# Two groups of the feed forward inside the drain of each attention layer, and the last two norms by a power on GpSimd

## The reference, cut to what matters

```
for l in range(2):
    h = shift_token(x)                                 # half the features come from the token before
    q, k, v = split(h @ wqkv[l])                       # 8 heads of 64
    o = local_attention(rotary(l2norm(q)), rotary(l2norm(k)), v)   # windows of 64 tokens
    x = x + o @ wo[l]
    h = shift_token(x)
    h = (h - mean) / sqrt(var + 1e-5) * ln_g[l] + ln_b[l]
    a, g = split(h @ w1[l] + b1[l])                    # 341 + 341 columns
    x = x + (a * gelu(g)) @ w2[l] + b2[l]
```

## Time and profile before

| | |
|---|---|
| median of 3 executions | 504.55 us (504.04 to 505.84) |
| profiled execution, its own time | 507.01 us |
| its span, first to last instruction | 505.1 us |
| PE busy | 435.7 us, 86% |
| weight loads | 302.5 us, 60% |
| DVE busy | 354.5 us, 70% |
| ACT busy | 313.4 us, 62% |
| POOL busy | 256.5 us, 51% |
| mean granted clock of PE | 0.947 |

### The profile page before, as it was taken

The page is one execution under the profiler, slowest core; times in us unless marked ns, Lnnn a source line. Parts: engine busy times, 40 slices in busy tenths (PEclk is TensorE's granted clock), DMA queues, the critical chain, the costliest instruction groups (busy, mean ns, idle before and its releaser), DMA issues.

```text
span 505.1 us, 13155 instructions
## 1 busy us (share of the span) xinstructions
PE 435.7 (86%) x4851; PEld 302.5 (60%) x4851; DVE 354.5 (70%) x733; ACT 313.4 (62%) x698; POOL 256.5 (51%) x225
## 2 busy tenths in 40 slices
PE   4899897749899999999885998989999999885993
PEld 2566565415677776766652665767667676672563
DVE  3687867265888888888642356689888898842556
ACT  2787676326677787877635244768778787651424
POOL 4578877465656666566440015565665656610002
PEclk9999899668999999999898999899999999989797
DMA  6900000000000000000000000000000000000002
GB/s 177 328 6 3 3 3 1 1 1 2 6 6 12 9 9 9 7 14 7 8 10 6 0 1 1 5 10 6 11 8 7 13 7 11 8 9 9 0 1 83
DMA packets 21038, 10.36 MB, mean 21 GB/s; under 512 B 13236, under 2 KB 20208, under 8 KB 20976
## 3 DMA queue, kind: packets, MB, share of 16 engines
q1 hardware_dynamic: 20400, 9.14, 6.7%
q10 hardware_dynamic: 576, 0.39, 0.2%
HBM read 6.38 MB, written 1.05 MB: 15 GB/s over the span
## 4 chain that ended last, share of the span: by engine, by line
PE 24%; DVE 23%; ACT 19%; issue 12%; POOL 3%; DMA 1%; SPq 0%; DVEq 0%; ACTq 0%; POOLq 0%
PE psum L534 19%; DVE ss L1497 7%; DVE neg_max L1514 7%; ACT sq L1131 6%; ACT qk_t L1150 4%; DVE probs L1521 3%; ACT probs_t L1163 3%; ACT probs L1156 2%; PE psum L792 2%; POOL qr L480 2%; ACT ln_z L1185 1%; DMA hcat<-middle 1%; PE psum L834 1%; DVE row_rec L1534 1%; DVE x_in L1440 1%
## 5 line engine op out<-in xcount | busy, mean ns | idle before, releaser
L471 POOL TENSOR_TENSOR qr<-rot 128x1024 f32<-128x1024 f32 x32 | 76.5, 2390 | 103.4 <-DVE rot L1489 103.4
L534 PE MATMUL psum<-wqkv_sb,h_t 128*128 128x512 f32 x192 | 98.5, 624 | 6.3 <-ACT sq L1131 4.2
L480 POOL TENSOR_TENSOR qr<-qr,inv 128x1024 f32<-128x1024 f32 x32 | 60.9, 1902 | 43.0 <-issue 38.6
L1497 DVE TENSOR_REDUCE ss<-sq 128x16 f32<-128x1024 f32 x32 | 39.0, 1219 | 37.3 <-ACT sq L1131 37.3
L534 PE MATMUL psum<-z_t,w_sb 128*128 128x512 f32 (+1 forms) x96 | 48.3, 639 | 1.2 <-ACT z_t L1196 1.1
L1156 ACT ACTIVATE probs<-probs 128x512 f32<-128x512 f32 x64 | 40.4, 631 | 13.1 <-DVE probs L1521 12.5
L534 PEld LDWEIGHTS psum<-wqkv_sb,h_t 128*128 128x128 f32 x192 | 33.1, 200 | 23.4 <-issue 20.9
L792 PEld LDWEIGHTS psum<-consts,qr 128*128 128x128 f32 x256 | 30.6, 144 | 26.5 <-POOL qr L480 13.7
L1521 DVE TENSOR_TENSOR probs<-psum,neg_max 128x512 f32<-128x512 f32 x64 | 44.2, 691 | 2.2
L1170 ACT ACTIVATE o_t<-psum 128x512 f32<-128x512 f32 x32 | 19.1, 598 | 41.9 <-PE psum L859 41.9
L1514 DVE TENSOR_REDUCE neg_max<-psum 128x4 f32<-128x512 f32 x64 | 43.5, 679 | 0.7 <-PE psum L534 0.6
(11 more groups left out here) (144 smaller groups left out, 941.0 us busy)
## 6 DMA issues: line engine op xcount, KB each, us to landing
wqkv_sb<-in_L_ffn_wqkv SPq DMA_DIRECT2D x1, 1536.0 KB, 9.4
hcat<-middle SPq DMA_DIRECT2D x32, 32.0 KB
out_x<-pong SPq DMA_DIRECT2D x8, 128.0 KB, 1.9
hcat<-middle SPq DMA_DIRECT2D x32, 31.8 KB
x_in<-in_L_attn_x SPq DMA_DIRECT2D x2, 384.0 KB, 4.2
w_sb<-in_L_ffn_w SPq DMA_DIRECT2D x1, 682.0 KB
cos_base<-rotary_cos SPq DMA_DIRECT2D x1, 512.0 KB, 5.1
sin_base<-rotary_sin SPq DMA_DIRECT2D x1, 512.0 KB, 6.0
```

What stands on the lines that cost most here:

```text
L471: pool.tensor_tensor(o, a, b[:, :, ::-1, :], ALU.add).then_inc(s["add_ready"], 1)
L480: pool.tensor_tensor(a, a, inv[:, :].unsqueeze(2).to_broadcast([P, 2 * AH, DH]), ALU.mult).then_inc(s["qr_ready"], 1)
L534: return pe.matmul(o, w, m, start=start, stop=stop, skip_group_check=skip)
L1497: dve.tensor_reduce(ss[:, :], sq[:, :].rearrange("p (h e) -> p h e", e=DH), AX.X, ALU.add).then_inc(s["ss_ready"], 1)
```

## The change

`feed_forward` is split on all three engines. It now takes the groups to run, and a table of stages to run beside block (g, j). A new `drain()` takes the place of steps 16 to 18: it runs groups 0 and 1 with the last stages of the attention between the blocks. Groups 2 and 3 run where the whole feed forward was, and `last_products` follows. Each group waits for its own four tiles only. Block (1, 0) moves from banks (0, 3) to banks (1, 2), and product (0, 0) waits for `copy_o_t` of the last tile in place of `hid` of block (1, 0). The load of the GELU table comes ahead of the last `copy_o_t` and of the last two `copy_z_t`.

For tiles 14 and 15, ACT's Ln and Exp are gone. DVE adds the epsilon to the variance, and POOL raises the sum to the power -0.5 (a column that DVE fills at the start).

```
 def block_banks(i):
-    return ((1, 2), (6, 7), (4, 5), (0, 3))[i] if i < 4 else ((6, 7), (4, 5))[i % 2]
+    return ((1, 2), (6, 7), (4, 5), (1, 2))[i] if i < 4 else ((6, 7), (4, 5))[i % 2]
...
 # POOL, behind its loop (and behind the tables of layer 1)
+    def rstd_of_z(n):
+        N = base + n
+        wait(pool, s["z_ln"], N + 1)
+        wait(pool, s["zn_ready"], N)
+        pool.tensor_tensor(rstd_z[:, :], ln_z[:, :], half_power, ALU.pow).then_inc(s["z_rstd"], 1)
...
+    pool.wait_ge(s["half_ready"], 1)
+    pool.wait_ge(s["vup_ready"], base + NT)
+    for n in (NT - 2, NT - 1):
+        rstd_of_z(n)
...
 # PE
 def hidden_block(m, g, j):
-    if b > 3:
+    if j == 0:
+        pe.wait_ge(s["z_ready"], NT * m + (g + 1) * GROUP)
+    if b >= 3:
         pe.wait_ge(s["hid_ready"], i - 1 if b > 5 else i - 2)
...
 def hidden_products(m, g, half):
     if (g, half) == (0, 0):
-        pe.wait_ge(s["hid_ready"], (G + 1) * NJ + 1)
+        pe.wait_ge(s["ot_ready"], NT * (m + 1))
...
+def drain():
+    last = NT - 1
+    def first_block():
+        transpose_z(last - 2, (last - 2) % 2)
+        if l == 0:
+            pe.wait_ge(d["d_ffn"], 16 * 7)
+        pe.wait_ge(s["rot_ready"], base + NT)
+        pe.wait_ge(s["sq_ready"], base + NT)
+    def second_block():
+        transpose_o(last, last % 2)
+        pe.wait_ge(s["pt0_ready"], base + NT)
+        pe.wait_ge(s["pt1_ready"], base + NT)
+    def third_block():
+        project_o(last, last % 2)
+        pe.wait_ge(s["on_ready"], base + NT)
+    feed_forward(l, (0, 1), {(0, 0): (first_block,), (0, 1): (second_block,), (0, 2): (third_block,),
+                             (1, 0): (lambda: transpose_z(last - 1, (last - 1) % 2),),
+                             (1, 2): (lambda: transpose_z(last, last % 2),)})
...
-iterate(pe, attn_step, first=-1, end=NT + 3, before={NT: early_blocks, NT + 1: last_early_block})
+iterate(pe, attn_step, first=-1, end=NT)
+drain()
...
 # ACT
+def drain():
+    last = NT - 1
+    copy_z_t(last - 2, (last - 2) % 2)
+    act.preload_act_table_set("gelu_and_others")
+    feed_forward(l, (0, 1), {(0, 1): (lambda: copy_o_t(last, last % 2),),
+                             (1, 0): (lambda: copy_z_t(last - 1, (last - 1) % 2),),
+                             (1, 2): (lambda: copy_z_t(last, last % 2),)})
...
 # DVE
+def variance_z(n, par):
+    N = base + n
+    wait(dve, s["z_aggr"], N + 1)
+    wait(dve, s["z_rstd"], N)
+    dve.tensor_scalar(ln_z[:, :], mv_z[:, 1:2], EPS, None, ALU.add).then_inc(s["z_ln"], 1)
+def normalised(n):
+    for stage in (stats_z, aggregate_z, variance_z, normalise_z):
+        stage(n, n % 2)
+def drain():
+    last = NT - 1
+    def last_outputs():
+        row_reciprocals(last, last % 2)
+        normalise_o(last, last % 2)
+    feed_forward(l, (0, 1), {(0, 0): (last_outputs,), (0, 1): (lambda: normalised(last - 1),),
+                             (0, 2): (lambda: add_attention(last, last % 2),), (1, 1): (lambda: normalised(last),)})
...
+feed_forward(DEPTH - 1, range(2, NG), {})
```

More of the change, by code:

```diff
@@ L723, in hidden_products, with feed_forward, last_products @@
                 ins.then_inc(s["h2_done"], 1)
-            def feed_forward(m, *first_tile):
-                pe.wait_ge(s["z_ready"], NT * (m + 1))
-                for g in range(NG):
+            def feed_forward(m, groups, beside):
+                for g in groups:
                     for j in range(NJ):
[L730 to L733, removed]
+                        for fn in beside.get((g, j), ()):
+                            fn()
+                        hidden_block(m, g, j)
                         if g > 0 and j > 0:
                             hidden_products(m, g - 1, j - 1)
+            def last_products(m):
                 hidden_products(m, NG - 1, 0)
@@ L919, in _ @@
                 if l:
-                    feed_forward(l - 1, enter, enter_on)
+                    feed_forward(l - 1, range(2, NG), {(NG - 2, 1): (enter,), (NG - 2, 2): (enter_on,)})
+                    last_products(l - 1)
                 else:
@@ L1096, in _, with feed_forward @@
             gla_o_t = copy_o_t
-            def feed_forward(m, *first_tile):
-                for g in range(NG):
+            def feed_forward(m, groups, beside):
+                for g in groups:
                     for j in range(NJ):
-                        if first_tile and (g, j) in ((NG - 2, 1), (NG - 1, 0), (NG - 1, 2)):
-                            first_tile[{(NG - 2, 1): 0, (NG - 1, 0): 1, (NG - 1, 2): 2}[g, j]]()
+                        for fn in beside.get((g, j), ()):
+                            fn()
                         i = (m * NG + g) * NJ + j
@@ L1221, in _ @@
                         stage(n, n % 2)
-                iterate(act, attn_step, first=-1, end=NT + 4)
-            feed_forward(DEPTH - 1)
+                iterate(act, attn_step, first=-1, end=NT)
+                drain()
+            feed_forward(DEPTH - 1, range(2, NG), {})
+            act.preload_act_table_set("natural_log_exp_and_others")
             bounds = [0] + list(range(NT - GROUP, NT + 1, 2))
@@ L1246, in _ @@
             dve.memset(norm_bias_col, 15 * LN2).then_inc(s["col_consts"], 1)
+            dve.memset(half_power, -0.5).then_inc(s["half_ready"], 1)
             dve.memset(state[:, 0:B * GDV], 0.0).then_inc(s["zero_state"], 1)
@@ L1458, in feed_forward, with out_of_first_groups @@
                             add_ffn(m, g - 1, j - 1)
[L1459 to L1473 removed]
+            def out_of_first_groups():
+                dve.wait_ge(s["rstdo_ready"], 1)
+                dve.scalar_tensor_tensor(out=shift_o[:, 0:NT - GROUP], in0=mv_o[:, 0:2 * (NT - GROUP):2], scalar=-1.0,
+                                         in1=rstd_o[:, 0:NT - GROUP], op0=ALU.mult, op1=ALU.mult
+                                         ).then_inc(s["shifto_ready"], 1)
+                for n in range(0, ON_ACT, 2):
+                    normalise_out(n)
             dve.wait_ge(d["d_cols"], 10 * 16)
@@ L1590, in _ @@
                         stage(n, n % 2)
-                iterate(dve, attn_step, first=-1, end=NT + 3)
-            feed_forward(DEPTH - 1)
+                iterate(dve, attn_step, first=-1, end=NT)
+                drain()
+            feed_forward(DEPTH - 1, range(2, NG), {})
+            out_of_first_groups()
+            add_ffn(DEPTH - 1, NG - 1, 0)
+            add_ffn(DEPTH - 1, NG - 1, 1)
             for n in range(NT - GROUP, NT, 2):
```

53 lines of the change are left out of this document (17 added, 36 removed).

## The result

| | before | after |
|---|---|---|
| median of 4 executions each | 505.16 us (504.04 to 505.84) | 487.02 us (484.67 to 487.86) |
| ratio | | 0.9635, 95% interval 0.9596 to 0.9675 |
| profiled execution, its own time | 507.01 us | 487.12 us |
| its span | 505.1 us | 485.1 us |
| mean granted clock of PE (1.00 is full speed) | 0.947 | 0.972 |

The kernel is faster by 3.65%, some 18 us; the forecast was 14.8 us and 489.7. The forecast lies outside what was measured. The experiments ask first whether the mechanism was the one forecast, then where the other 3 us are.

The account below looks back on a forecast made before the run. Tile 15's serial norm was taken to set each drain, with group 1's blocks waiting by code order. Gains of 7.25 and 7.55 us, 14.8 together, moved the median from 504.55 to 489.7 us; range 487.0 to 495.5.

Parts of the forecast that it names:

- PE's floor of 14.8: PE's work in a drain in the new order, transposes, projection, six blocks and two products: 14.8 us at least.
- The walk: First drain step by step: tile 15's transpose can start at 273.3, PE idles 0.7, drain 15.5 us instead of 22.75.
- The power: POOL's power for tiles 14 and 15: 0.5 us taken, range 0.1 to 1.25; beyond 0.5 it counts twice a drain.
- A first use of several us: Rival: POOL's first power is slow, costing its length in the first drain plus a clock fall; chance 0.03.
- The table load costs nothing: ACT's GELU table load lies beside block (0, 0) in the drain; without that cover it would cost 1.28 us.
- The clock did not fall at the wait: Rival: PE's clock falls at the wait left in a drain, 2.2 us each: 491.9 or 494.1 us; chance 0.14.
- The power was not slow: Rival: POOL's power takes 1 to 3 us, each us counting four times in all: 493.7 at 1.5; chance 0.10.
- ACT did not reload for copies: Rival: ACT reloads its table around the two `z_t` copies, 0.5 to 2 us a drain, 491 to 494; chance 0.06.
- POOL did not decide: Rival, slower kernel: POOL's power decides from 3.1 us on while DVE stands blocked, 508 at 4 us; chance 0.03.
- A fall costs 5.63 against 3.44: Price of a clock fall on two blocks in a drain: 2.2 us.
- the transfers take 0.65 longer, so 16.15: Second drain: longer transfers after `middle` make it 16.15 us instead of 23.71, 7.55 gained.
- no wait in either drain: Lower end of the forecast's own band: PE never waits in the drains, 7.95 + 8.9 us gained, 487.7.

Follow-up runs that it names:

- clock held up: Kernel before, with three products of no use to the result added in PE's wait for the last norm of each layer: median 502.12 us, ratio 0.995.
- the better of two runs: Changed order with Ln and Exp left on ACT, two table loads a norm instead of three, against the kernel before: median 493.51 us, ratio 0.9799.
- The three comparisons: Kernel after, unedited, measured three times against the kernel before: medians 487.02, 488.54 and 488.04 us, ratios 0.9635, 0.9653 and 0.969.

## Why the prediction was right in its steps and short in its sum

**What bound the drain: right.** The norm of tile 15 set it, and the blocks waited by order of the code alone. With the new order and the power, and PE's work the same, a drain goes from 22.6 (clock held up) to 15.4. The new order alone doesn't get there: with Ln and Exp left between the GELUs the drain is 18.3 in the better of two runs.

**PE's floor of 14.8: right**, 14.77 with the last transpose at the drain's end.

**The walk: right.** Each step came within 0.15 us of where it was put; the wait, a difference of two of them, was 0.48 in place of 0.7, and the first drain 15.40 in place of 15.5.

**The power: right in size and in that it counts twice**, 0.55 for the 0.5 taken, and 1.03 a drain when doubled. A first use of several us was not shown: the first power took 0.567 to 0.568 in each of the three profiled executions. What it took in executions that were not profiled, no run shows.

**The table load costs nothing: right**, to 0.1 us. Still four loads behind the first; block (0, 0) covers the one of the drain, and the first GELU starts 0.02 us behind the load's end.

**The rivals.** The clock did not fall at the wait of 0.48, nor in the experiments at 1.20, 1.43 and 1.67 (granted clock 1.00 in those drains); it did at 2.94 (0.64 behind it). The power was not slow, early or late; ACT did not reload for copies; POOL did not decide. One price in them was wrong: "A fall costs 5.63 against 3.44". In the old drain those two blocks take 5.27 without any fall, since PE waits for `hid` between them. In the new order, where a fall came (Ln and Exp with three loads), it cost 1.69 in the drain, not 2.2.

**The sum failed: what the two drains give was put too low, and what lies outside them was left out.** The steps, in the prediction's own terms:

1. *The second drain's transfers.* The step "the transfers take 0.65 longer, so 16.15" took a difference seen once, 4.82 against 4.17, for a property of that drain. They took 4.16, and the drain 15.38. This term is off by 0.77, and the first drain's by 0.10. Of the six drains in the three profiles of the kernel before, one had 4.82 and the others 4.15 to 4.17; what made that one longer is not shown.
2. *The old drains.* "22.75" and "23.71" were subtracted as if fixed. Over three profiles their sum was 45.5 to 48.2, and 46.7 on average, 0.3 more than in the one used. With the clock held up it would be 45.1. So of the 16.0 that the drains gave by the profiles, 14.4 us is the order with the power, and 1.6 is the clock that no longer falls.
3. *The rest.* "Behind either drain nothing changes place" is right, but the rest of one program moved by up to 6.8 us between profiles. The sum had no term for it, and the range's lower end allowed only "no wait in either drain" and nothing for this. The first comparison has four executions a kernel; its 487.02 is the lowest of the three medians of the kernel after, whose 14 executions together have 487.7. To that extent the size of the miss is chance.

The first two make 16.0 us, not 14.8: 46.7 less 30.8. The three comparisons, by their ratios and 505 us, give 18.4, 17.5 and 15.7 us, 17.2 on average. So 16.0 lies within the intervals of the second and third, and 0.4 us short of the first's (0.9596 to 0.9675, that is 16.4 to 20.4 us). Of the profiled pair's 20.0 us, 15.7 are the drains and 4.3 the rest. The latter came from stretches such as 245 to 250, which had a granted clock of 0.70 in the old profile, where the two attentions of the new one ran at 0.99 to 1.00. In three profiles a kernel, the rests average 454.9 before and 454.4 after.

That leaves 1.2 of the 17.2 us. The kernel before with its clock held up helps to place it: its median, 502.12, stands 14.4 us above the 487.7 of the kernel after, just what their drains differ by (45.1 less 30.8). So nothing is left over between those two, and the 1.2 most likely belongs to the clock of the kernel before, which the medians put at 2.5 us (1.2 to 3.8) and three profiles of its drains at 1.6. Whether it fell in the drains of executions that were not profiled or in their rest, no run shows.

## What to carry to other kernels

Where a serial chain ends a loop, put work that already has its inputs ahead of each of its waits, in program order, and see what stands between that work on every other engine: here the new order was worth 1 us a drain with seven table loads in it, 5 with five and 8 with one. A small function on an idle engine need not be faster than the one it replaces, if it leaves the other engine's table alone: here the power took 0.55 us, Ln and Exp 0.49, and in the new order it still saved 2.9 us a drain against two table loads a norm. And build a sum from more than one execution, or give the range a term for what one program's executions differ by: here 8 us of span between three profiles, nearly half of what the change gave.

## What the runs showed of the hardware

- A PE wait of the same length, 3.5 us, was followed by two blocks of 5.3 to 7.0 us. When the clock fell, and for how much of the work behind, differed from one execution to the next, so a fall has no fixed price.
- Waits of 1.20 to 1.67 us in an otherwise busy drain left the granted clock at 1.00 (drains of 16.4 and 18.3 us). Behind waits of 2.71 and 2.94 us in one drain, only the second was followed by a fall: 4.75 us from block (1, 2) to block (2, 0) at a granted clock of 0.64, 3.06 at 1.00.
- Between the GELUs, Ln and Exp of one norm got a table load each, 1.28 us; with the set that holds both named ahead they had one between them. An ACTIVATE that had its input started within 0.02 us of the load's end.
- A power of 128x1 on POOL took 0.55 to 0.57 us, and in the kernel after DVE stood for 0.66 to 0.83 between handing it over and going on.
- From the end of `middle` of tile 15 to DVE's statistics, with three transfers between, it was 4.15 to 4.17 us in 11 of the 12 drains of the kernels before and after, and 4.82 in one.
